# A state-space layer's output projection for five of eight groups, from fp32 matmuls to three products of rounded halves

## What is computed

```python
proj = hidden_states @ in_proj_w.T          # gate (8192), x, B, C (10240), dt (128)
xc   = silu(causal_conv(hBC, conv_w, taps=4) + conv_b)
M    = (C B^T) * exp(segment_sum(A * dt))   # per head, 128 heads of 64 channels
y    = M @ (x * dt) + D * x                 # 8192 channels
y    = y * rsqrt(mean(y ** 2) + eps) * norm_w * silu(gate)
out  = y @ out_proj_w.T                     # 8192 -> 512: the output projection
```

## Time and profile before

| | |
|---|---|
| median of 3 runs | 638.62 us (638.28 to 638.98) |
| the profiled execution | 638.21 us, of which the span from first to last instruction is 636.5 |
| PE busy | 623.0 us (98% of the span) |
| DVE busy | 434.4 us (68%) |
| ACT busy | 337.5 us (53%) |
| POOL busy | 212.9 us (33%) |
| bytes moved | 116.69 MB, mean 183 GB/s |

### The profile page before, as it was taken

The page is one execution under the profiler, slowest core; times in us unless marked ns, Lnnn a source line. Parts: engine busy times, 40 slices in busy tenths (PEclk is TensorE's granted clock), DMA queues, the critical chain, the costliest instruction groups (busy, mean ns, idle before and its releaser), DMA issues.

```text
span 636.5 us, 11116 instructions
## 1 busy us (share of the span) xinstructions
PE 623.0 (98%) x3968; PEld 531.6 (84%) x3968; DVE 434.4 (68%) x885; ACT 337.5 (53%) x617; POOL 212.9 (33%) x161
## 2 busy tenths in 40 slices
PE   8999999999999999999999989999999999999998
PEld 6888887888999899889998879998879778797573
DVE  3533135686777777778876669789884775958873
ACT  3413114668776777777777636656454454447110
POOL 0000000349676867687765522225022020200000
PEclk9999999999999999999999999999999999999999
DMA  8501012467777767776756939475866757697500
GB/s 265 214 0 34 1 55 66 103 176 205 191 192 191 190 165 179 188 203 156 214 137 168 355 133 267 160 304 195 295 210 255 265 204 262 246 367 289 217 1 18
DMA packets 29534, 116.69 MB, mean 183 GB/s; under 512 B 7680, under 2 KB 8064, under 8 KB 21936
## 3 DMA queue, kind: packets, MB, share of 16 engines
q1 hardware_dynamic: 28912, 115.03, 57.7%
q10 hardware_dynamic: 576, 1.05, 0.6%
HBM read 86.30 MB, written 0.26 MB: 136 GB/s over the span
## 4 chain that ended last, share of the span: by engine, by line
PE 84%; DVE 6%; issue 2%; ACT 2%; DMA 2%; SPq 2%; POOL 1%; ACTq 0%; DVEq 0%
PE ps L1716 20%; PE ps L1434 13%; PE ps L1436 12%; PE ps L1435 12%; PE ps L1756 9%; PE ps L1508 4%; PE ps L1591 2%; PE ps L1745 2%; PE ps L1866 2%; DVE prob_far L1081 2%; DMA ring<-ctx_t_dram 2%; SPq L351 2%; PE ps L1829 2%; DVE prob_far L1109 2%; DVE res L1121 1%
## 5 line engine op out<-in xcount | busy, mean ns | idle before, releaser
L1716 PEld LDWEIGHTS ps<-norm_t,ring 128*128 128x128 f32 x1152 | 131.6, 192 | 4.9 <-issue 4.1
L1716 PE MATMUL ps<-norm_t,ring 128*128 128x128 f32 x1152 | 133.2, 276 | 0.0
L507 POOL TENSOR_TENSOR pt_lo<-far_t,pt_hi 128x512 fp32r<-128x512 f32 x86 | 102.2, 1203 | 61.6 <-ACT pt_hi L609 61.3
L1265 DVE SCALAR_TENSOR_TENSOR acc<-raw,cw,acc 128x127 f32<-128x127 f32 (+2 forms) x240 | 83.4, 424 | 18.8 <-ACT acc L879 18.2
L1081 DVE TENSOR_SCALAR_CACHE_REDUCE prob_far<-ps 128x1024 f32<-128x1024 f32 x64 | 73.8, 1155 | 31.9 <-PE ps L1436 31.6
L686 ACT ACTIVATE prob_far<-prob_far,neg_max 128x1024 f32<-128x1024 f32 x64 | 69.8, 1091 | 25.7 <-DVE neg_max L1085 25.6
L609 ACT ACTIVATE pt_hi<-far_t 128x512 fp32r<-128x512 f32 x90 | 51.3, 587 | 36.7 <-PE ps L1436 33.9
L1109 DVE STREAM_TRANSPOSE prob_far<-prob_far 128x1920 f32<-128x1920 f32 x30 | 65.0, 2171 | 0.1
L1434 PE MATMUL ps<-k_hi,q_hi 128*128 128x512 f32 (+2 forms) x160 | 62.4, 390 | 2.0 <-DVE prob_far L1081 1.6
L1434 PE MATMUL ps<-pt_hi,v_hi 128*128 128x256 f32 x208 | 61.1, 294 | 2.1 <-POOL pt_lo L507 1.2
L583 POOL TENSOR_SCALAR_AFFINE_SELECT at_hi<-a_hi 128x2048 fp32r<-128x2048 f32 x8 | 16.1, 2011 | 133.9 <-PE ps L1728 102.8
(11 more groups left out here) (213 smaller groups left out, 1213.8 us busy)
## 6 DMA issues: line engine op xcount, KB each, us to landing
ring<-w_in_dram SPq DMA_DIRECT2D x36, 1024.0 KB, 4.9
far_t<-prob_far SPq DMA_DIRECT2D x240, 120.0 KB, 2.3
ring<-w_out_dram SPq DMA_DIRECT2D x16, 1024.0 KB, 4.8
ring<-wq_dram SPq DMA_DIRECT2D x16, 512.0 KB, 4.2
ring<-wo_dram SPq DMA_DIRECT2D x16, 512.0 KB, 3.6
w_sb<-w_dram SPq DMA_DIRECT2D x4, 896.0 KB, 9.1
ring<-ctx_t_dram SPq DMA_DIRECT2D x3, 1024.0 KB, 6.9
ring<-w_dram SPq DMA_DIRECT2D x3, 1024.0 KB, 7.5
```

Source lines behind the costliest of these rows:

```text
L507: sub = lambda dst, a, hi: pool.tensor_tensor(dst, a, hi, ALU.subtract)
L1265: ins = nc.vector.scalar_tensor_tensor(a[:, i, back:], r[:, i, 0:T - back], cw[:, bass.ds(tile + i, 1), 3 - back:4 - back].rearrange("p a ...
L1716: ins = mm(ps[:, bank, t * T:t * T + T], w[:, t, c, :], norm_t[:, c, :], start=(c == 0), stop=(c == NC - 1))
```

## The change

The output projection of groups 0 to 4 runs as three fp32r products; groups 5 to 7 keep fp32. ACT makes the high halves: `ug_hi` in `gated_round(g)` and `out_hi` (of a ring slot) in `out_round(g, i)`. DVE makes the low halves in place, in `gated_low(g)` and `out_low(g, i)`. The DVE and PE loops over steps are written out; ACT's loop stays. `ug_lo` and `ring_lo` lie where `ug` and the ring slot lie; `out_hi` and `ug_hi` lie in memory that `w1` fills later.

```diff
@@ ACT
+            def out_round(g, i):
+                slot, before = out_chunk(g, i)
+                act.wait_ge(landed[slot], (before + 1) * 16)
+                copy(out_hi[i][:], ring[slot][:].rearrange("p (t n) -> p t n", t=4)).then_inc(outh_ok, 1)
+            def gated_round(g, b):
+                act.wait_ge(ug_ok, 2 * g + 2)
+                copy(ug_hi[b][:], ug[b][:]).then_inc(ugh_ok, 1)
...
             copy(c2_st[:], c2_sb[:]).then_inc(c2h_ok, 1)
+            gated_round(0, 0)
+            out_round(0, 0)
...
-            def mamba_step(g, b, last=False):
+            def mamba_step(g, b, split_out, split_next, last=False):
                 k, o = 2 * g + 6, 1 - b
                 decay_exp(g + 1, o, 0)
+                if split_out:
+                    out_round(g - 1, 1)
                 raw_out(step_chunk(g, 0), k, 0, 8 * g + 8)
...
+                if split_next:
+                    gated_round(g, b)
+                    out_round(g, 0)
                 gate_out(step_chunk(g, 3), 1, sg[o][:, 4:8, :])
...
-                    mamba_step(turn * 2 + (i + 1), 1 - i)
-            mamba_step(5, 1)
-            mamba_step(6, 0, True)
+                    mamba_step(turn * 2 + (i + 1), 1 - i, True, True)
+            mamba_step(5, 1, True, False)
+            mamba_step(6, 0, False, False, True)
@@ DVE
+            def gated_low(g, b):
+                dve.wait_ge(ugh_ok, g + 1)
+                sub(ug_lo[b][:], ug[b][:], ug_hi[b][:].bitcast(F32)).then_inc(ugl_ok, 1)
+            def out_low(g, i):
+                slot = out_chunk(g, i)[0]
+                dve.wait_ge(outh_ok, 2 * g + i + 1)
+                sub(ring_lo[slot][:].rearrange("p (t n) -> p t n", t=4), ring[slot][:].rearrange("p (t n) -> p t n", t=4),
+                    out_hi[i][:].bitcast(F32)).then_inc(outl_ok, 1)
...
             add_squares(0)
+            gated_low(0, 0)
+            out_low(0, 0)
...
                 mask_decay(g + 1, o, 0)
+                if g <= ROUNDED:
+                    out_low(g - 1, 1)
                 taps_of(q, k, 0, 8 * g + 8)
...
                 add_squares(g)
+                if g < ROUNDED:
+                    gated_low(g, b)
+                    out_low(g, 0)
@@ PE
+            def split_out_proj(g, b, i, first=False):
+                slot = out_chunk(g, i)[0]
+                pe.wait_ge(ugl_ok, g + 1)
+                pe.wait_ge(outl_ok, 2 * g + i + 1)
+                w_lo_ = ring_lo[slot][:].rearrange("p (t n) -> p t n", t=4)
+                for t in range(4):
+                    ins = split_product(ps[:, 6, :], ug_hi[b][:, 4 * i + t, :], ug_lo[b][:, 4 * i + t, :],
+                                        out_hi[i][:, t, :], w_lo_[:, t, :], first and i == 0 and t == 0, False)
+                ins.then_inc(freed[slot], 1)
...
-                out_proj(before_g, 1 - b, 0, first)
-                out_proj(before_g, 1 - b, 1)
+                for i in range(2):
+                    if before_g < ROUNDED:
+                        split_out_proj(before_g, 1 - b, i, first)
+                    else:
+                        out_proj(before_g, 1 - b, i)
```

More of the change, by code:

```diff
@@ L81 @@
 LN_STEPS = 8
+ROUNDED = 5
 WARM = 12
@@ L233, in build @@
                 sq_tok = sbuf(st4, "sq_tok", [P, 2, T])
-                ug = [sbuf(st4, f"ug{b}", [P, TPG, T]) for b in range(2)]
+                ug, ug_lo = [], []
+                for b in range(2):
+                    with ExitStack() as same_place:
+                        ug_lo.append(sbuf(same_place, f"ug_lo{b}", [P, TPG, T], F32R))
+                    ug.append(sbuf(st4, f"ug{b}", [P, TPG, T]))
                 at_hi.append(sbuf(st4, "at_hi1", [P, HPG, T], F32R))
@@ L239, in build @@
                     w1_lo = sbuf(same_place, "w1_lo", [P, NC, FF], F32R)
+                with ExitStack() as same_place:
+                    out_hi = [sbuf(same_place, f"out_hi{i}", [P, 4, DM], F32R) for i in range(2)]
+                    ug_hi = [sbuf(same_place, f"ug_hi{b}", [P, TPG, T], F32R) for b in range(2)]
                 w1_sb = sbuf(st4, "w1_sb", [P, NC, FF])
@@ L287, in build @@
         ug_ok, var_s = sem("ug_ok"), sem("var_s")
+        outh_ok, outl_ok, ugh_ok, ugl_ok = sem("outh_ok"), sem("outl_ok"), sem("ugh_ok"), sem("ugl_ok")
         f_mask = sem("f_mask")
@@ L1335, in _ @@
             add_squares(0)
+            gated_low(0, 0)
+            out_low(0, 0)
             def mamba_step(g, b):
                 q, k, o = 4 * g + 8, 2 * g + 6, 1 - b
-                if not (isinstance(g, int) and g == 1):
+                if g > 1:
                     x_times_dt(g)
                 mask_decay(g + 1, o, 0)
+                if g <= ROUNDED:
+                    out_low(g - 1, 1)
                 taps_of(q, k, 0, 8 * g + 8)
@@ L1347, in mamba_step @@
                 add_squares(g)
[L1349 to L1353, removed]
+                if g < ROUNDED:
+                    gated_low(g, b)
+                    out_low(g, 0)
+            for g in range(1, GROUPS - 1):
+                mamba_step(g, g % 2)
             def w1_split(c):
@@ L1747, in y_product, with out_proj @@
                 ins.then_inc(y_ps, 1)
-            def out_proj(g, b, i, first=False, last=False):
+            def out_proj(g, b, i, last=False):
                 slot, before = out_chunk(g, i)
@@ L1755, in out_proj @@
                 for t in range(4):
-                    ins = mm(ps[:, 6, :], ug[b][:, 4 * i + t, :], w[:, t, :], start=(first and i == 0 and t == 0),
+                    ins = mm(ps[:, 6, :], ug[b][:, 4 * i + t, :], w[:, t, :], start=False,
                              stop=(last and i == 1 and t == 3))
+                ins.then_inc(freed[slot], 1)
[7 more added lines that the diff above has]
+                                        out_hi[i][:, t, :], w_lo_[:, t, :], first and i == 0 and t == 0, False)
                 ins.then_inc(freed[slot], 1)
@@ L1792, in mamba_step @@
                 project(g, 1)
-                out_proj(before_g, 1 - b, 0, first)
-                out_proj(before_g, 1 - b, 1)
+                for i in range(2):
[3 more added lines that the diff above has]
+                        out_proj(before_g, 1 - b, i)
                 project(g, 2)
                 project(g, 3)
[L1798 to L1802, removed]
+            for g in range(1, GROUPS - 1):
+                mamba_step(g, g - 1, g % 2, g == 1)
             x_transposes(7, 1)
```

## The result

| | before | with the change |
|---|---|---|
| median | 638.62 us (638.28 to 638.98) | 641.63 us (640.38 to 642.81, 5 runs) |
| ratio | | 1.0045, 95% interval 1.0029 to 1.0060 |
| the profiled execution | 638.21 us, span 636.5 | 641.06 us, span 639.3 |

The change made the kernel slower by 3.0 us; the forecast was 6.0. Part 1 of the page of the changed kernel, busy us of each engine, shows what the change paid for and what it got: 3.7 us less on PE, 32.9 more on DVE, 22.2 more on ACT and 11.0 more on POOL, which got no new work. Time in which an instruction is held by another engine counts as busy.

A forecast was written before the change was run, and what follows sets the result against it. PE, busy in all of each 26.0 us step, was taken as the bound; 4.0 + 2.7 + 2.1 + 3.4 - 6.15 = +6.0 us gave 644.6 us, own range 642.5 to 646.5, whole range 638.2 to 647.4.

The forecast's parts named there:

- PE's saving: Output projection in steps 1 to 5: three matmuls replace two fp32 records, 1.23 us less a step, 6.15 us in all.
- The first wait: Step 1: PE waits for the decay, delayed on ACT by `gated_round(0)` and `out_round(0, 0)`; +4.0 us.
- The second wait: Start of step 2: `x_transposes(2)` waits for the second `conv_silu`, behind DVE's taps that POOL holds up; +2.7 us.
- The single row that was set beside the taps: DVE's `pt_lo`: 1.77 us beside POOL's `wo_lo`, 0.69 alone; taken to show that POOL holds such subtractions.
- The rival of the clock: Step 1: PE's 4 us wait lowers its clock, costing up to 2.75 us; 645.6 us, at worst 647.4; chance 0.14.
- a sign of being wrong: Step 1: the forecast would be wrong if the granted clock fell below 1 between 437 and 445 us.
- the bound of 2.75: PE's largest loss at the lower clock after step 1's wait: 5.49/2 us, from the kernel's first 24 matmuls.
- The third wait: Step 2: PE's second segments wait for ACT's copies, table load and decay after the gate, until 469.05, not 466.9; +2.1 us.
- The loop: Steps 3 to 5: gate to gate through ACT, DVE and POOL takes 25.9 us against PE's 24.77; +3.4 us.
- Not held: Rival: POOL doesn't hold DVE's added subtractions, so the loop is some 23.2 us; +0.3 us, 638.9 us; chance 0.13.
- POOL for nothing: Rival: POOL costs DVE next to nothing, PE sets every step; -2.15 us, 636.5 us; chance 0.07.
- The written-out loops at nothing: DVE and PE loops: removing register instructions and branches gains nothing, as DVE idles 3.48 us before its next step in step 3.

The follow-up runs named there:

- the filled wait: The changed kernel with 17 idle matmuls put into PE's wait of step 1, POOL as in the change: 641.47 us, ratio 1.0041 to the kernel before.
- the run with only `c2` moved: The changed kernel with POOL's subtraction on `c2` moved from step 1 to step 6, its masked copies left in place: 637.71 us, ratio 0.9981.
- the run with the rounding behind the decay: The changed kernel with ACT's three copies behind the next step's first decay and DVE's three subtractions behind its mask, POOL unchanged: 637.87 us, ratio 0.9985.

## Why the prediction came out too high

*PE's saving: right.* It is 1.33 us a step, forecast 1.23.

*The first wait: right.* It is 4.12 us, forecast 4.0, at the place named, behind the copies named.

*The second wait: right in place and size, with some luck, and the trace of the change doesn't show it as a wait.* Step 2 was to begin 30.22 us behind the start of the `c2` copy (431.38 to 461.6) and begins 30.12 behind it. DVE behind POOL and PE at the low clock end together there; the filled wait shows DVE's alone. But in step 1 it is `ring_lo` that holds POOL, where the forecast had POOL holding `ring_lo`: at the low clock POOL starts 2.14 us behind the second segments instead of 1.27. Since the two run one behind the other in either order, the gate still ends 0.3 us from where it was forecast. The single row that was set beside the taps was also misread in one point: DVE's `pt_lo`, from 351.75, stands behind POOL's own `pt_lo`, which runs until 352.98, and not behind `wo_lo`, which starts at 352.93. It shows a hold all the same.

*The rival of the clock: came true in its condition, not in its time.* The granted clock fell below 1 between 437 and 445, which the prediction had named as a sign of being wrong. By itself that costs 2.9 us, a little more than the bound of 2.75. The bound took the first 24 matmuls of the kernel for matmuls at the lower level; the trace of the kernel before shows no granted clock under 1.00 there, so that is not shown. The prediction let some of the cost lie in the second wait; nearly all of it does (0.4 us is left).

*The third wait: right in place.* The second segments of step 2 start 37.32 us behind the copy's start, forecast 37.67; PE waits 1.67 us there, forecast 2.1.

*The loop: right in kind, mis-sized, and this is the step that failed in the changed part.* "This loop, not PE's 24.77, now sets the step: 1.13 us of waiting in steps 3, 4 and 5, +3.4." It does set the step, by the pieces named, but in 25.35 us instead of 25.9, so 0.58 a step over 24.77: 1.7 us instead of 3.4. From the gate's end to the end of the second `out_hi` it is 7.5 us where 7.87 had been summed, `ring_lo` takes 3.95 where 4.23 was the hold and the work, and the taps take 4.9 where it was 5.2; the rest of the turn is 9.0 where it was 8.8. Full durations were added one behind the other, with 0.2 us taken off for overlaps in the whole turn, at a place where each of ACT's instructions overlaps its neighbour by 0.1; and POOL's first masked copy ended 9.35 us behind the gate instead of 9.8, which freed DVE sooner. With 0.35 us from step 2, that is 2.0 of the 6.0 forecast: the stretch shows +4.05.

*Not held, and POOL for nothing: wrong.* `ring_lo` at 3.94 us rejects both.

*The written-out loops at nothing: the second step that failed, its cause open.* The stretch alone would have given 638.62 + 4.05 = 642.7 us, just inside the prediction's own range of 642.5 to 646.5. The rest, down to +3.0 between the medians, lies ahead of the changed steps: in the profiled execution the `c2` copy starts at 430.20 us instead of 431.38. The prediction costed the written-out loops at nothing from what DVE does in step 3; what the runs show of them is in the first loads, 400 us earlier. How much of the 1 us is theirs and how much is scatter of that part is not settled.

## What to carry to other kernels

Work that fits into the pauses of an engine by its sum can still form a loop through several engines: add up one turn of it, from one event to the same event a step later, with what each instruction waits for on the ports, and compare that with the step of the bound engine. Where such a loop is only some tenths of a us longer than the step, its start counts as much as its length: in the run with only `c2` moved, a gate 3.9 us earlier at the start bought three steps without waits and most of a fourth. And where two causes end at the same place, as in step 1, removing either shows little there: remove both. Here it paid to put the rounding copies behind the operation that the bound engine waits for, and not ahead of it.

## What the runs showed of the hardware

- In the change PE had nothing to do from 434.12 to 438.24 us, and the granted clock read 0.62 in the microsecond from 437, 0.50 until 444, 0.96 in the microsecond from 444 and 1.00 behind it; the matmuls of `y_product` took 3.68 us instead of 1.97. In the 3.92 us of waiting in the run with the rounding behind the decay it fell too (0.90 over step 2). Idle matmuls in the wait kept it at 1.00.
- POOL is held by DVE as DVE is by POOL: 3.79 us for a masked copy of 2.01, 4.05 for one that starts while `ring_lo` runs, and 5.95 for the subtraction of 3.97 where a `ring_lo` ran beside it (rounding behind the decay). Of a row of short DVE operations, one waits behind each POOL instruction: 2.09, 2.08 and 4.19 us for the first three taps of step 1, 0.34 for each of the others.
- The issue of the first four loads on ACT's queue took 2.8 us in two profiles of the kernel before and 1.96 to 2.05 us in the twelve with PE's loop written out, with the same loads.
